# A graph network kernel: edge weights in two scaled 16-bit float parts, and two groups of transfers at other places

## The chip, the cores and the metric

The kernel runs on one core of one Trainium2 chip. The time is device microseconds (us) of one execution, taken in several runs; the number compared is the median. A separate execution was recorded by the hardware profiler, and all rows below come from it.

## What is computed

There are 1250 nodes of 1024 features and 20,000 edges (sorted by destination) with a weight each. Two layers follow one another:

```
h   = relu(layernorm(x))
e   = sigmoid(h @ wenc.T + benc)                      # 1250 x 500
agg = segment_sum((e @ wconv)[src] * weight, dst)     # weighted adjacency times g
x   = x + (agg + e @ wlin.T) @ wdec.T + bdec
h1  = relu(layernorm(x))
z   = h1 @ W.T + b                                    # 1024 x 1024
x   = x + D^-1/2 (A + I) D^-1/2 z                     # A from the edges, unweighted
```

## The kernel before, in words

One core runs five engines from one list of steps that the function schedule() (L138) writes out by hand. Each engine walks through the same list and emits its own part of each step, so the order of steps is the order of work of every engine and of SP's queue of transfers. Semaphores tie the engines together. Nodes are tiled by 128 (10 tiles) and, for the encoder, in 5 blocks of 256.

**Opening.** SP (L688 to L695) loads the heads of the edge rows, six tiles of x, wenc and benc. ScalarE counts where each row of edges starts (L956), GpSimd gathers the edge rows with an indirect transfer (L880). VectorE computes the statistics, ScalarE the norms (L971), TensorE turns the tiles (L1714) and multiplies them with wenc (L1739, L1576 to L1578). Products are made of high and low parts: `product` (L1574) issues three matmuls.

**Edge fields.** On ScalarE the step "parts" (L1049) and on VectorE "fields" (L1239) make of each edge a key (place in a window), the low part of the source and three bf16 parts W1, W2, W3 of the weight, which add up to the f32 weight. TensorE turns the five fields (L1677) into the banks wbank[0], wbank[1] and one of the six dense banks; ScalarE (L1059) and VectorE (L1260) copy them out, each value twice, to kkey, skey and wq.

**Windows.** 50 windows of 25 destinations, each of 5 sub-windows, make the adjacency by matmuls. For window w VectorE ("hot", L1264) compares iotas with kkey and skey, which gives one-hot matrices o_key and o_src, and multiplies the keys with the WPARTS parts of the weight (L1280). TensorE ("win", L1686) then issues for each sub-window, with o_src as the stationary operand:

```
o (100 columns)  += o_src x [ones part | W1 part]     # L1694
o[:, 50:100]     += o_src x W2 part                   # L1696
o[:, 50:100]     += o_src x W3 part                   # L1698
```

ScalarE copies the counts to cnt and the weighted values to stage (L1067, L1070); SP stores stage to adj_scratch in DRAM (L701). Window w on TensorE waits for the stage copy of window w-2 (L1690). The windows are mixed into the dense steps by their due times (L200 to L230): two windows after each encoder group ("e", b, f) from block 1 on, then after each tile of g = e @ wconv ("g", t), then after the first two wlin products ("swl", 0, f). ScalarE and VectorE have their own evacuations and norms beside them, named in `beside` (L182).

**Scales.** Weights and wconv are scaled by powers of two before they become 16-bit parts. The steps ("size", "ew") and ("size", "wc") (L982, L986) sum absolute values on ScalarE, ("limits", "out") and ("limits", "in") send them over DRAM to all partitions (L748, L751), and ("limits", "scale") (L1317) makes the scales on VectorE. The scale of the weights is applied when the adjacency is read back, in "unit" (L1097, L1413).

**W1.** W (the second layer) is sized too: eight tiles of 512 KB are loaded through two buffers (L733) and summed on ScalarE (L978). The list puts sizes 0 to 6 after g tiles 1, 2, 3, 6, 9 and the first two wlin products, the last size at step (1, 1), and the step "bounds" at (1, 5).

**Aggregation.** The 1250 destinations are done in three thirds (500, 500, 250). SP loads the adjacency rows of a third into the one buffer raw ("piece" L786 for the first, "raw" L796 for the others; a load waits until all ten units of the third before are made). ScalarE and VectorE make of each source tile k a pair of 16-bit parts, a unit (ring of 6), and TensorE multiplies it with g ("sk", L1804), after the wlin products of that third. Beside the first third ScalarE and VectorE count degrees (L990, L1430), and SP turns the ten tiles of cnt with turning transfers ("flip", L809). The degree row goes out to DRAM and back ("row", L800) for the row sums of the second third (L1488). The step ("raw", 1) stands behind the last flip.

After that come the decoder, the second layer norm, and the second layer with its own products; the change leaves them alone.

Of the kernel before, what the change touches and what calls it, by code (L numbers as in the profile page):

```python
# [17 lines left out]
P = 128  # L18
T = 10
# [29 lines left out]
WPARTS = 3  # L49
# [15 lines left out]
EW_ROWS = 125.0  # L65
# [8 lines left out]
KEY, SLO, W1, W2, W3 = range(5)  # L74
# [63 lines left out]
def schedule():  # L138
# [35 lines left out]
    steps += [third[3]] + lo(e[1], t1[1], t1[2], t1[3]) + [e[2], ("fields",)] + lo(e[2]) + [("load", "ew"), ("load", "wc"), e[3]] + norms(2)[1:]  # L174
# [3 lines left out]
    def both(block):  # L178
# [4 lines left out]
        (1, 0): turn(2)[:2] + fourth[1:3] + turn(2)[2:], (1, 1): fourth[3:], (1, 2): [("size", "ew"), ("norm", 6)] + fifth[:1], (1, 3): [("norm", 7), ("split", 6), ("turn", 6)],  # L183
# [29 lines left out]
    for i, s in enumerate(dense + [("end",)]):  # L213
        while stream and i >= begin and (stream[0][0] * total <= spent * NW or s[0] == "end"):
            if stream[0][1] == ("hot", 0):

                steps += [("lo", *g) for g in late]
                late = []
# [7 lines left out]
        if s[0] in ("e", "g", "t", "edges") and not by_dma(s):  # L226
            late += [s]
# [7 lines left out]
    for n in range(NS):  # L235
# [4 lines left out]
        for k in range(T):  # L240
# [19 lines left out]
        if n + 1 < NS:  # L260
# [41 lines left out]
def build(nc, x, edge_rows, heads_dst, nat_src, nat_dst, nat_w,  # L302
# [4 lines left out]
    limit_row = nc.dram_tensor("limit_scratch", (P, 2), F32).ap()  # L307
# [17 lines left out]
    for s in STEPS:  # L325
# [7 lines left out]
        elif s[0] in ("t", "e", "g", "z", "edges"):  # L333
# [32 lines left out]
    with ExitStack() as ctx:  # L366
# [23 lines left out]
        kkey = small("kkey", [128, ROWS, 2], BF16)  # L390
        skey = small("skey", [128, ROWS, 2], BF16)
        wq = small("wq", [128, ROWS, WPARTS, 2], BF16)
        iota_s = small("iota_s", [128, 128], BF16)
        a2_rest = at("a2_rest", [P, T, B], F16, 0)
        dis_row = at("dis_row", [P, NODESP], F32, 0)
        assert top[0] >= T * B * 2
        iota_k = small("iota_k", [128, WC], BF16)
# [3 lines left out]
        lane = small("lane", [128, 128], F32)  # L401
# [18 lines left out]
        sizes = small("sizes", [P, 2], F32)  # L420
# [25 lines left out]
        R_X = R_OX + (RING * SUB * (256 + 8 * KC) + 31) // 32 * 32  # L446
        R_END = R_X + 4 * 4096
# [10 lines left out]
        o_key = at("o_key", [128, RING, SUB, 1 + WPARTS, KC], BF16, R_OX + RING * SUB * 256)  # L458
# [1418 lines left out]
```

## Time and profile before

| | us |
|---|---|
| median of 3 runs | 463.74 |
| lowest, highest | 461.7, 467.1 |
| the profiled execution, its own time | 462.57 |
| its span, first to last instruction | 460.8 |
| TensorE busy in it | 451.3 (98%) |
| VectorE, ScalarE busy in it | 309.9 (67%), 239.8 (52%) |

Busy time is the union of an engine's instructions; the ends of matmuls are modelled and overlap the next ones, so the start of the next matmul says more than the duration of one. A row of the timeline has start, duration, engine, line, operation, output and input with shapes, and in brackets how long the engine sat idle before it and what ended that. DMA rows of SP's queue are the issue of a transfer, not the transfer.

### The profile page before, as it was taken

How to read it: one execution, taken by the hardware profiler on the slowest of the kernel's cores; microseconds unless marked ns; L12 is line 12 of the kernel's file. 1: busy time of each engine (PE TensorE's matmuls, PEld its weight loads, DVE VectorE, ACT ScalarE, POOL GpSimd, SP SyncE). 2: the span in 40 equal slices, each digit the busy share in tenths (PEclk: the TensorE clock that was granted, in tenths of full speed). 3: DMA queues.
4: the chain of work that ended last, by engine and by line, in shares of the span. 5: the costliest groups of instructions: out<-in, count | busy, mean ns of one | idle time of the engine just before them, and what ended most of it. 6: DMA issues, size and time to landing. Idle time of an engine off the chain costs nothing.

```text
span 460.8 us, 9335 instructions
## 1 busy us (share of the span) xinstructions
PE 451.3 (98%) x3452; PEld 341.2 (74%) x3452; DVE 309.9 (67%) x603; ACT 239.8 (52%) x452; POOL 42.5 (9%) x63
## 2 busy tenths in 40 slices
PE   7999999998999998999999999999999999999997
PEld 5999999987876455449888887888889944444454
DVE  6999897975965322965867777848563556667652
ACT  6987896639769823314434444546644722222220
POOL 3511200000000000000000000266500000000000
PEclk9999999999999999999999999999999999999999
DMA  8850965297545799143730004350659004423433
GB/s 306 271 179 24 159 104 126 73 342 251 182 152 117 144 80 378 63 123 103 288 102 0 2 0 140 136 183 1 246 212 360 7 1 160 138 91 117 155 134 113
DMA packets 48402, 66.42 MB, mean 144 GB/s; under 512 B 25793, under 2 KB 35024, under 8 KB 46820
## 3 DMA queue, kind: packets, MB, share of 16 engines
q1 hardware_dynamic: 48036, 65.39, 46.7%
q8 instruction: 32, 0.52, 0.5%
q0 software_dynamic: 320, 0.39, 0.4%
q14 instruction: 14, 0.11, 0.1%
HBM read 43.62 MB, written 16.77 MB: 131 GB/s over the span
## 4 chain that ended last, share of the span: by engine, by line
PE 89%; DMA 5%; ACT 2%; SPq 2%; issue 1%; DVE 0%; POOL 0%; POOLq 0%
PE bank L1576 21%; PE bank L1577 20%; PE bank L1578 20%; PE bank L1592 19%; DMA raw<-adj_scratch 3%; PE bank L1694 2%; DMA w_tile<-w 2%; PE bank L1714 1%; SPq L817 1%; PE bank L1739 1%; PE bank L1696 1%; PE bank L1698 1%; DMA adj_scratch<-stage 1%; ACT before L956 1%; PE bank L1654 1%
## 5 line engine op out<-in xcount | busy, mean ns | idle before, releaser
L1592 PE MATMUL bank<-a,h_hi 128*128 128x256 f16 (+3 forms) x400 | 85.5, 270 | 0.0
L1592 PE MATMUL bank<-a,h_lo 128*128 128x256 f16 (+3 forms) x400 | 85.5, 270 | 0.0
L1576 PE MATMUL bank<-right,left 128*128 128x512 f16 (+1 forms) x148 | 54.4, 367 | 0.0
L1578 PE MATMUL bank<-right,left 128*128 128x512 f16 (+1 forms) x148 | 54.4, 367 | 0.0
L1577 PE MATMUL bank<-right,left 128*128 128x512 f16 (+1 forms) x148 | 54.4, 367 | 0.0
L1146 ACT CAST left<-zs 128x512 f16<-128x512 f32 x35 | 21.5, 617 | 60.3 <-PE bank L1578 60.3
L1561 DVE SCALAR_TENSOR_TENSOR x<-bank,dis_u,x 128x512 f32<-128x512 f32 (+2 forms) x37 | 26.7, 722 | 34.2 <-PE bank L1578 34.2
L1576 PE MATMUL bank<-unit,g 128*128 128x500 f16 (+3 forms) x120 | 40.8, 340 | 2.1 <-DVE unit L1418 2.1
L1592 PEld LDWEIGHTS bank<-a,h_hi 128*128 128x128 f16 (+1 forms) x400 | 38.9, 97 | 4.2 <-issue 0.3
L1592 PEld LDWEIGHTS bank<-a,h_lo 128*128 128x128 f16 (+1 forms) x400 | 39.1, 98 | 3.8
L1576 PE MATMUL bank<-h0T,we 128*128 128x256 f32 (+3 forms) x144 | 41.3, 287 | 0.0
L1578 PE MATMUL bank<-unit,g 128*128 128x500 f16 (+3 forms) x120 | 40.7, 339 | 0.0
L1577 PE MATMUL bank<-unit,g 128*128 128x500 f16 (+3 forms) x120 | 40.7, 339 | 0.0
L1577 PE MATMUL bank<-h0T,we 128*128 128x256 f32 (+3 forms) x144 | 40.3, 280 | 0.0
L1578 PE MATMUL bank<-h0T,we 128*128 128x256 f32 (+3 forms) x144 | 40.2, 279 | 0.0
L1418 DVE SCALAR_TENSOR_TENSOR unit<-raw,scales,unit 128x500 f16<-128x500 f32 (+1 forms) x30 | 18.7, 651 | 23.1 <-ACT unit L1106 23.1
L1548 DVE SCALAR_TENSOR_TENSOR right<-whole,o_scales,right 128x512 f16<-128x512 f32 x28 | 26.6, 1014 | 8.7 <-ACT right L1154 8.7
L1576 PE MATMUL bank<-wd_hi,hT 128*128 128x512 f32 (+1 forms) x80 | 31.7, 396 | 0.0
L1577 PE MATMUL bank<-wd_lo,hT 128*128 128x512 f32 (+1 forms) x80 | 31.6, 395 | 0.0
L1106 ACT ACTIVATE unit<-raw,scales 128x500 f16<-128x500 f32 (+1 forms) x30 | 18.5, 650 | 25.1 <-PE bank L1578 14.3
L1578 PE MATMUL bank<-wd_hi,hT 128*128 128x512 f32 (+1 forms) x80 | 31.4, 393 | 0.0
L1694 PE MATMUL bank<-o_key,o_src 128*128 128x100 bf16 x250 | 27.8, 206 | 1.4 <-ACT stage L1070 1.4
(188 smaller groups left out, 1060.5 us busy)
## 6 DMA issues: line engine op xcount, KB each, us to landing
whole<-w SPq DMA_DIRECT2D x7, 1024.0 KB, 7.4
adj_scratch<-stage SPq DMA_DIRECT2D x50, 125.0 KB, 2.1
right_scratch<-right SPq DMA_DIRECT2D x5, 1024.0 KB, 4.0
right<-right_scratch SPq DMA_DIRECT2D x5, 1024.0 KB, 4.8
h<-x SPq DMA_DIRECT2D x9, 512.0 KB, 5.9
x<-x SPq DMA_DIRECT2D x9, 512.0 KB, 5.3
out<-x SPq DMA_DIRECT2D x18, 256.0 KB
w_tile<-w SPq DMA_DIRECT2D x8, 512.0 KB, 5.3
```

What stands on the lines that cost most here:

```text
L817: sp.dma_start(a2[:, :, P * k:P * (k + 1)], cnt[:, k, :], transpose=True).then_inc(flipped, 16)
L956: ins = nc.scalar.activation(before[:, c, :], firsts[:], ACT.Sign, bias=heads[:, c:c + 1])
L1106: nc.scalar.activation(units[0][:, u % UNITS, 0:c].rearrange("p (w d) -> p w d", d=W), raw[:, 0:c // W, k, :], ACT.Copy, scale=scale_of[1] ...
L1146: nc.scalar.copy(left[0][:, nth[p, b] % LEFTS, :, :], side(b, PRODUCTS[p][0])).then_inc(left_hi, 1)
L1418: v.scalar_tensor_tensor(units[1][:, u % UNITS, 0:c].rearrange("p (w d) -> p w d", d=W), raw[:, 0:c // W, k, :], scale_of[1], units[0][:, ...
L1548: v.scalar_tensor_tensor(right[slot_of(i)][1][:, k, :], whole[slot_of(i)][:, k, :], w1_scale, right[slot_of(i)][0][:, k, :], ALU.mult, ALU ...
L1561: v.scalar_tensor_tensor(xs, bank[banks_of[g]][0:n, 0:c.stop - c.start], dis_u[0:n, t:t + 1], xs, ALU.mult, ALU.add).then_inc(bank_free, 1)
L1576: pe.matmul(o, lhs[0], rhs[0], start=first, stop=False, skip_group_check=True)
L1577: pe.matmul(o, lhs[0], rhs[1], start=False, stop=False, skip_group_check=True)
L1578: return pe.matmul(o, lhs[1], rhs[0], start=False, stop=last, skip_group_check=True)
L1592: ins = pe.matmul(o, h1[i][0:n, k, 128 * f:128 * (f + 1)], moving, start=(k == 0 and part == 0 and i == 0), stop=(k == T - 1 and part == p ...
L1694: pe.matmul(o, o_src[:, r, i, :], o_key[:, r, i, 0:2, :], start=(i == 0), stop=False, skip_group_check=True)
```

## The change

- WPARTS is 2: the weight is multiplied by its scale first and then split in two 16-bit float parts. kkey, wq, iota_k and o_key are 16-bit float, o_src and skey stay bf16. The third matmul of each sub-window goes, and so do the fifth turned field, its dense bank and its copy on VectorE.
- The scale of the weights is therefore needed before the fields. The weights are loaded behind the second tile of x; ScalarE sums them before its first norm; SP stores the sums, waits, and loads them to all partitions before its list of steps begins; a step "weights" on VectorE makes the scale, and one on ScalarE the high part. The units use a constant factor instead of the scale. The limits of wconv stay where they were, half as large.
- ("raw", 1) stands in step (0, 7), ahead of ("degrees",), ("row", "out") and flips 7, 8 and 9; flip 7 was before issued with the earlier ones. ("raw", 2) stays.
- W1's sizes 0 to 4 follow g tiles 2, 4, 6, 8 and the first wlin product; sizes 5, 6, 7 stand at steps (1, 1), (1, 2), (1, 3), with the load of the last tile at (1, 1).

```diff
-WPARTS = 3
+WPARTS = 2
...
-    steps += [third[3]] + lo(e[1], t1[1], t1[2], t1[3]) + [e[2], ("fields",)] + lo(e[2]) + [("load", "ew"), ("load", "wc"), e[3]] + norms(2)[1:]
+    steps += [third[3]] + lo(e[1], t1[1], t1[2], t1[3]) + [e[2], ("weights",), ("fields",)] + lo(e[2]) + [("load", "wc"), e[3]] + norms(2)[1:]
...
-    for k, s in enumerate([("g", 1), ("g", 2), ("g", 3), ("g", 6), ("g", 9), *opening[:2]]):
+    for k, s in enumerate([("g", 2), ("g", 4), ("g", 6), ("g", 8), opening[0]]):
         i = dense.index(s) + 1
-        dense[i:i] = [("size", "w1", k)] + [("load", "w1", k + 2)] * (k + 2 < KD)
+        dense[i:i] = [("size", "w1", k)] + [("load", "w1", k + 2)]
...
                 for d in DEGREES[k]:
-                    steps += [("degree", d)] + ([("flip", d)] if d < T - 2 else [])
+                    steps += [("degree", d)] + ([("flip", d)] if d < T - 3 else [])
             if (n, k) == (0, 7):
-                steps += [("degrees",), ("row", "out"), ("flip", T - 2), ("flip", T - 1)]
+                steps += [("raw", 1), ("degrees",), ("row", "out"), ("flip", T - 3), ("flip", T - 2), ("flip", T - 1)]
             if (n, k) == (1, 0):
                 steps += [("row", "in"), ("load", "wd")]
-            if (n, k) == (1, 1):
-                steps += [("size", "w1", KD - 1)]
+            if n == 1 and k in (1, 2, 3):
+                steps += [("size", "w1", KD - 4 + k)] + [("load", "w1", KD - 2 + k)] * (k == 1)
...
-        if n + 1 < NS:
+        if n == 1:
             steps += [("raw", n + 1)]
...
                 sp.dma_start(h0[t][0:tile_rows(t), :], rows(x, t)).then_inc(x_in[t], 16)
+                if t == 1:
+                    sp.dma_start(ew_raw[:], nat_w).then_inc(ew_in, 16)
...
             sp.dma_start(benc_c[:], benc).then_inc(benc_in, 16)
+            sp.wait_ge(ew_sized, 1)
+            sp.dma_start(ew_row, ew_sizes[:]).then_inc(ew_out, 16)
+            sp.wait_ge(ew_out, 16)
+            sp.dma_start(all_limits[:, 0:EP], ew_row.rearrange("q i -> (q i)").unsqueeze(0).broadcast_to([P, EP])).then_inc(ew_sizes_in, 16)
...
             ins.then_inc(before_ready, 1)
+            act.wait_ge(ew_in, 16)
+            nc.scalar.activation(ew_raw[:], ew_raw[:], ACT.Abs, accum_out=ew_sizes[:]).then_inc(ew_sized, 1)
...
-                    nc.scalar.copy(fld[:, W1, :, :], edges[:, :, 2, :].bitcast(F32))
...
+                elif s[0] == "weights":
+                    act.wait_ge(ew_scale_ready, 1)
+                    nc.scalar.activation(weights[:, 0, :, :], edges[:, :, 2, :].bitcast(F32), ACT.Copy, scale=scale_of[1][0:EP, :]).then_inc(weights_hi, 1)
...
-                                         ACT.Copy, scale=scale_of[1]).then_inc(unit_hi, 1)
+                                         ACT.Copy, scale=UNIT_SCALE).then_inc(unit_hi, 1)
...
+                elif s[0] == "weights":
+
+                    dve.wait_ge(ew_sizes_in, 16)
+                    link(v.tensor_reduce(limits[:, 1:2], all_limits[:, 0:EP], AX, ALU.max))
+                    link(v.tensor_scalar(limits[:, 1:2], limits[:, 1:2], LEAST, None, ALU.max))
+                    link(v.tensor_scalar(scales[:, 1:2], limits[:, 1:2].bitcast(I32), EXP_MASK, None, ALU.bitwise_and))
+                    v.tensor_scalar(scales[:, 1:2], scales[:, 1:2], -1.0, float((HALF_EXP + 254) * EXP_ONE), ALU.mult, ALU.add).then_inc(ew_scale_ready, 1)
+                    dve.wait_ge(ew_scale_ready, 1)
...
-                    v.tensor_tensor(r, wt, f[W1], ALU.subtract)
-                    v.tensor_copy(f[W2], r)
-                    v.tensor_tensor(f[W3], r, f[W2], ALU.subtract)
...
-                    v.scalar_tensor_tensor(f[KEY], a, 1.0, sf, ALU.add, ALU.mult).then_inc(fields_ready, 1)
+                    v.scalar_tensor_tensor(f[KEY], a, 1.0, sf, ALU.add, ALU.mult)
+                    dve.wait_ge(weights_hi, 1)
+                    v.scalar_tensor_tensor(weights[:, 1, :, :], wt, scale_of[1][0:EP, :], weights[:, 0, :, :], ALU.mult, ALU.subtract).then_inc(fields_ready, 1)
...
-                        pe.matmul(o[:, KC:2 * KC], o_src[:, r, i, :], o_key[:, r, i, 2, :], start=False, stop=False,
-                                  skip_group_check=True)
-                        ins = pe.matmul(o[:, KC:2 * KC], o_src[:, r, i, :], o_key[:, r, i, 3, :], start=False, stop=(i == SUB - 1),
+                        ins = pe.matmul(o[:, KC:2 * KC], o_src[:, r, i, :], o_key[:, r, i, 2, :], start=False, stop=(i == SUB - 1),
                                         skip_group_check=True)
```

## Rows read from the trace of the kernel before

**Rows 1.** The page, part 1: busy us, share of the span, instructions.
```profile
PE 451.3 (98%) x3452; PEld 341.2 (74%) x3452; DVE 309.9 (67%) x603; ACT 239.8 (52%) x452; POOL 42.5 (9%) x63
```

**Rows 2.** Waits of TensorE: engine, line, waited for: us, times, longest.
```profile
PE bank L1576 <- DVE unit L1418: 2.1, 1, 2.1
PE bank L1694 <- ACT stage L1070: 1.4, 1, 1.4
```

**Rows 3.** TensorE's timeline in two windows: start us, us, line, op.
```profile
45.95 0.22 PE L1694 MATMUL bank<-o_key,o_src 128*128 128x100 bf16 x1
46.00 0.19 PE L1696 MATMUL bank<-o_key,o_src 128*128 128x50 bf16 x1
...
46.06 0.20 PE L1694 MATMUL bank<-o_key,o_src 128*128 128x100 bf16 x1
...
46.45 0.20 PE L1694 MATMUL bank<-o_key,o_src 128*128 128x100 bf16 x1
```

**Rows 4.** TensorE's groups by form: count | busy us, mean ns.
```profile
L1696 PE MATMUL bank<-o_key,o_src 128*128 128x50 bf16 x250 | 27.0, 187 | 0.0
```

**Rows 5.** ScalarE's timeline, 50 to 71 us.
```profile
50.09 0.47 ACT L1039 ACTIVATE hT<-bank,benc_c 128x256 fp32r<-128x256 f32 x1 [1.30 <-PE bank L1578]
...
61.22 0.47 ACT L1070 COPY stage<-bank 128x250 f32<-128x250 f32 x1
...
70.11 0.47 ACT L1039 ACTIVATE hT<-bank,benc_c 128x256 fp32r<-128x256 f32 x1 [1.78 <-PE bank L1578]
```

**Rows 6.** TensorE's timeline, starts of windows 10 and 19.
```profile
61.74 0.22 PE L1694 MATMUL bank<-o_key,o_src 128*128 128x100 bf16 x1
...
78.25 0.20 PE L1694 MATMUL bank<-o_key,o_src 128*128 128x100 bf16 x1
```

**Rows 7.** VectorE's timeline, 77 to 82 us.
```profile
77.56 0.55 DVE L1280 TENSOR_TENSOR o_key<-o_key,wq 128x750 bf16<-128x750 bf16 x1
...
80.47 0.42 DVE L1319 TENSOR_REDUCE limits<-all_sizes 128x2 f32<-128x256 f32 x1
80.92 0.17 DVE L1320 TENSOR_SCALAR limits<-limits 128x2 f32<-128x2 f32 x1
```

**Rows 8.** Timeline of the opening: SP's queue, ScalarE, VectorE, TensorE.
```profile
6.17 0.62 SPq L695 DMA_DIRECT2D benc_c<-benc  x1
...
9.66 2.38 ACT L971 ACTIVATE h<-h,nbias,rstd 128x1024 f32<-128x1024 f32 x2 [2.86 <-DVE nbias L1236]
...
26.24 0.41 DVE L1245 TENSOR_TENSOR er<-edges,fld 125x256 f32<-125x256 f32 x1
...
29.80 0.42 DVE L1256 SCALAR_TENSOR_TENSOR fld<-er,er 125x256 bf16<-125x256 f32 x1
...
30.86 0.72 PE L1679 MATMUL bank<-identb,fld 125*128 125x125 bf16 x10
```

**Rows 9.** DMA issues by line: count, KB each, median us to landing.
```profile
raw<-adj_scratch SPq DMA_DIRECT2D x1, 2500.0 KB, 12.8
...
all_sizes<-limit_scratch SPq DMA_DIRECT2D x1, 128.0 KB, 3.7
...
benc_c<-benc SPq DMA_DIRECT2D x1, 2.0 KB, 13.3
```

**Rows 10.** Timeline around the first W1 size: SP's queue, ScalarE.
```profile
96.04 1.77 SPq L739 DMA_DIRECT2D w_tile<-w  x2
...
103.66 1.06 ACT L981 ACTIVATE w_tile<-w_tile 128x1024 f32<-128x1024 f32 x1 [4.73 <-DMA w_tile<-w]
```

**Rows 11.** Timeline between first and second third: VectorE, SP's queue.
```profile
157.37 0.74 DVE L1418 SCALAR_TENSOR_TENSOR unit<-raw,scales,unit 128x500 f16<-128x500 f32 x1 [0.39 <-ACT unit L1106]
...
167.76 0.58 SPq L685 DMA_DIRECT2D raw<-adj_scratch  x1
...
172.16 0.32 SPq L804 DMA_DIRECT2D dis_row<-row_scratch  x1
...
184.64 1.45 DVE L1494 SCALAR_TENSOR_TENSOR weighted<-cnt,dis_row 128x1250 f16<-128x1250 f16 x1
```

More of the change, by code:

```diff
@@ L73 @@
 EPS = 1e-5
-KEY, SLO, W1, W2, W3 = range(5)
+KEY, SLO, W1, W2 = range(4)
 NODESP = P * T
@@ L182, in schedule @@
     beside = {
-        (1, 0): turn(2)[:2] + fourth[1:3] + turn(2)[2:], (1, 1): fourth[3:], (1, 2): [("size", "ew"), ("norm", 6)] + fifth[:1], (1, 3): [("norm", 7), ("split", 6), ("turn", 6)],
+        (1, 0): turn(2)[:2] + fourth[1:3] + turn(2)[2:], (1, 1): fourth[3:], (1, 2): [("norm", 6)] + fifth[:1], (1, 3): [("norm", 7), ("split", 6), ("turn", 6)],
         (2, 0): [("split", 7), ("turn", 7)] + fifth[1:], (2, 1): [("size", "wc")], (2, 2): both(turn(3)) + [("norm", 8)],
@@ L215, in schedule @@
             if stream[0][1] == ("hot", 0):
-                steps += [("lo", *g) for g in late]
+                steps += [("lo", *g) for g in late] + [("missed",)]
                 late = []
@@ L225, in schedule @@
                 spent += s[0] in ("e", "g", "swl")
-        if s[0] in ("e", "g", "t", "edges") and not by_dma(s):
+        if s[0] in ("e", "g", "t") and not by_dma(s):
             late += [s]
@@ L395, in build @@
         dis_row = at("dis_row", [P, NODESP], F32, 0)
+        iota_k = small("iota_k", [128, WC], F16)
+        lane = small("lane", [128, 128], F32)
         assert top[0] >= T * B * 2
-        iota_k = small("iota_k", [128, WC], BF16)
         ident = small("ident", [128, 128], F32)
@@ L419, in build @@
         minus_half = small("minus_half", [P, 2], F32)
-        sizes = small("sizes", [P, 2], F32)
+        sizes = small("sizes", [P, 1], F32)
+        ew_sizes = small("ew_sizes", [EP, 1], F32)
         w1_sizes = small("w1_sizes", [P, KD], F32)
@@ L462, in build @@
         edges = at("edges", [EP, RG, 3, ROW], I32, R_RAW)
-        er = [at(f"er{i}", [EP, RG, ROW], F32, R_RAW + 3072 + 1024 * i) for i in range(5)]
-        fld = at("fld", [EP, 5, RG, ROW], BF16, R_RAW + 3072 + 1024 * 5)
+        er = [at(f"er{i}", [EP, RG, ROW], F32, R_RAW + 3072 + 1024 * i) for i in range(4)]
+        fld = at("fld", [EP, 2, RG, ROW], BF16, R_RAW + 3072 + 1024 * 5)
+        weights = at("weights", [EP, WPARTS, RG, ROW], F16, R_RAW + 3072 + 1024 * 6)
         heads_i = at("heads_i", [EP, HC], I32, R_RAW + 10752)
@@ L485, in build @@
         gen16 = at("gen16", [EP, CH], BF16, R_H0T + 16384 + 640 * 15)
-        gen_src = [at(f"gen_src{i}", [EP, 128], BF16, R_OX + 256 * i) for i in range(1 + WPARTS)]
+        gen_src = [at(f"gen_src{i}", [EP, 128], BF16, R_OX + 256 * i) for i in range(4)]
         gen_key = at("gen_key", [EP, WC], BF16, R_OX + 1024)
@@ L1676, in _ @@
                     pe.wait_ge(idents, 2)
-                    for i, (o, c) in enumerate(((wbank[0], 0), (wbank[0], ROWS), (wbank[1], 0), (wbank[1], ROWS), (take(s), 0))):
+                    for i, (o, c) in enumerate(((wbank[0], 0), (wbank[0], ROWS), (wbank[1], 0), (wbank[1], ROWS))):
                         for j in range(RG):
-                            ins = pe.matmul(o[:, c + EP * j:c + EP * (j + 1)], fld[:, i, j, :], identb[0:EP, 0:EP],
-                                            start=(c == 0 and j == 0), stop=True, skip_group_check=True)
-                        if i == 3:
-                            ins.then_inc(fields_turned, 1)
+                            if i < W1:
+                                ins = pe.matmul(o[:, c + EP * j:c + EP * (j + 1)], fld[:, i, j, :], identb[0:EP, 0:EP],
+                                                start=(c == 0 and j == 0), stop=True, skip_group_check=True)
+                            else:
+                                ins = pe.matmul(o[:, c + EP * j:c + EP * (j + 1)], weights[:, i - W1, j, :], ident16[0:EP, 0:EP],
+                                                start=(c == 0 and j == 0), stop=True, skip_group_check=True)
                     ins.then_inc(acc_ready, 1)
```

70 lines of the change are left out of this document (32 added, 38 removed).

## The prediction

> **What bounds the kernel now.** I read the page first, then the waits of TensorE, then the timelines around each of those waits. The page gives TensorE 451.3 us busy in a span of 460.8 us, VectorE 309.9 and ScalarE 239.8 [rows 1]. So the time is the length of TensorE's stream plus its few holes: whatever shortens that stream, or closes a hole, counts one for one unless another engine catches up. The waits of TensorE have two holes past the opening: 2.1 us for a unit of the adjacency and 1.4 us for a staged window [rows 2]. Busy time is no price for a small matmul, since the ends overlap: a 50-column one shows as 187 ns [rows 4], but by the starts inside a window the 100-column one takes 50 ns and the two 50-column ones 60 ns together, and a whole window of five such sub-windows 0.50 us (45.95 to 46.45) [rows 3]; so one of 50 columns is 25 to 30 ns. I price matmuls by starts.
>
> **One matmul of each sub-window less.** The window step issues three matmuls per sub-window, the change two: 250 of the form of L1696 go [rows 4]. 250 x 27 ns = 6.75 us, 0.135 us per window. Ends: 25 ns each is 6.2 us, 30 ns is 7.5 us. The stationary stays bf16 and the moving operand becomes 16-bit float; no product with two different 16-bit formats is in this trace, so its rate is bounded by the 27 ns above and by twice that (a rival below). The page "TensorE: Matmul & The Clock Gate" of the Trainium skill (Back-to-back issue gap) puts a stream of weight load and matmul pairs at about 81 ns per matmul at 128 columns; by that the edit would be worth 20 us. The trace disagrees with it: the 100-column matmul takes 50 ns to the next start [rows 3], so the sum does not use it.
>
> Not all of that is kept. Window w waits for the stage copy of window w-2 on ScalarE. Between 50.1 us, where ScalarE waited 1.30 us for TensorE, and 68 us it never waits again until the 1.78 us at 70.11 [rows 5]: it is behind, and the stage copy of window 8 ends at 61.69, 0.05 us before window 10 starts [rows 5, 6]. A faster TensorE only waits there. Windows 4 to 11, eight of them, buy nothing: 8 x 0.135 = 1.1 us off. Then at window 19 VectorE is what is late: its key operation begins at 77.56 and takes 0.55, the window starts at 78.25 [rows 6, 7]. That VectorE work hangs on ScalarE's catch-up, so it moves forward less than TensorE does; 0.45 us off. Kept: 6.75 - 1.1 - 0.45 = 5.2 us. If ScalarE's lag spreads to later blocks the floor is 3.5; if its stretch loosens the ceiling is 6.75.
>
> VectorE's product of keys and weights has 750 elements at 0.55 us [rows 7], once per window. With 500 it should lose up to a third less a fixed part, some 0.13 us each, 6.5 us in all, beside TensorE: priced at nothing except that it keeps VectorE from becoming the next bound. Of the ten turning matmuls of the fields (0.72 us shown for the group [rows 8]) two go: 0.1 us. The copy of the third part on VectorE goes too, in the shade of the wait for ScalarE's copies.
>
> **The opening.** Added: a load of the weights (78 KB) behind two rows of x, an Abs pass on ScalarE, a store and a broadcast load on SP, five operations on VectorE, one on ScalarE. The Abs (under 0.5 us) falls into ScalarE's 2.86 us wait before the first norm at 9.66 [rows 8]; what waits behind it is that norm. It costs something only if the load lands after about 9. The store queues behind all of the opening's loads: the small benc load, issued last at 6.17 [rows 8], took 13.3 us, to about 19.5 us, and the broadcast of the limits took 3.7 [rows 9]. So the broadcast should land at 23 to 24.5; SP stands until then minus 4, and behind it stand the loads of x rows 6 and 7, whose statistics come only after the fields. VectorE gets to the weights at 26.24 [rows 8], some 2 us later than needed. The block of fields took 26.24 to 30.2 [rows 8]. Three operations leave it (about 0.9 us); the reduction and three linked small ones come (a reduction twice as long took 0.42, a small one 0.17 [rows 7], with links about 1.1 us in all), and one more at the end (0.35): fields ready about 0.6 us later, against TensorE's own arrival at 30.86 [rows 8]. I take 0.1 us of new wait. Ends: 0, and 1.5 us if the broadcast comes 1 us late. The page "DMA: Bandwidth & Descriptors" of the Trainium skill (How many engines) says a transfer of 125 partitions runs on 5 of the 16 engines; then 78 KB would hold five of them half as long as an x row does and push the first half of wenc by about 0.6 us. No row here shows it; it would stay inside the 1.5 us.
>
> **W1's sizes later.** The 1.4 us hole at 106 us has this chain: SP issues the W1 tiles at 96.04, ScalarE comes to size the first at 98.93, waits 4.73 us to 103.66 [rows 10], copies the next g bank and only then the windows, and TensorE's window 32 waits for stage 30 [rows 2]. The first size now stands one g tile later (3.8 us): ScalarE reaches it at about 102.7 and waits 1 us, done by 104.8, while the stage that TensorE needs next is already written. Gain 1.4 us (ends 0 and 1.4). Two of the seven sizes leave this stretch, so ScalarE begins the units about 1.1 us sooner. The last three go into the second third; the last tile's load stands behind the 2 MB of wd, so ScalarE may stand until about 190, but the unit behind it is used only at the eighth step. Cost 0; if that cover is gone, whatever the load is late.
>
> **Second third's rows earlier.** SP issued the load at 167.76 [rows 11], behind two turning transfers and the store of dis; it took 12.8 us to land [rows 9], so the next unit could begin at 180.6, and TensorE resumed at about 182.3 after its wait of 2.1 us [rows 2]. Its own condition, the tenth unit on VectorE, was met at 158.1 [rows 11]. Issued then, and given the same 12.8 us, it lands at 171, against a need at about 178.5: 2.1 us saved, ends 0 and 2.1. Three turning transfers and the store of dis are now behind 2.5 MB. The row load (dis_row) was issued at 172.16 [rows 11]; with the big load out of the queue before it I expect about 176, landing before 184. The first row sum ran at 184.64 [rows 11] and the sixth unit of this third queues behind it on VectorE; TensorE wants that at about 192.8 (five steps of 2.5 us from 180.1). Nothing lost.
>
> **Sum.** 5.2 + 0.1 + 1.4 + 2.1 - 0.1 = 8.7 us. The profiled execution took 462.57 us: 453.9. The median of the three runs is 463.74, 1.2 above it (461.7 to 467.1): I forecast 455.0 us. A measurement of this kernel tells about 1%, 4.6 us, from no change.
>
> **Rivals.**
> 1. A hole stays (0.24). One of the two waits does not close: the W1 tile lands later relative to the shortened stream, or the load of rows shares the engines with the turning transfers. For it: the W1 tiles issued at 96.04 were there only at 103.66 [rows 10]. Against: both moves have 1 to 7 us of room. Price 1.4 to 2.1, or up to 3.5: 456.5 to 458.5.
> 2. Windows worth less and a new wait (0.12). ScalarE's lag reaches past 70 us and the opening or the dis_row chain adds 1 to 2 us. Against: ScalarE waits 1.78 us at 70.11 [rows 5]. Gain 2 to 4.5: 459.3 to 461.7.
> 3. The mixed product is slow (0.05), the other side. A bf16 stationary with 16-bit float moving at half rate: a sub-window would take 2 x (50 + 27 - 3) = 148 ns instead of 98, a window 0.25 us more, fifty 12.5 us; with the 3.5 of the holes 9.0 longer: 472.7. It decides from about 0.07 us more per window, where it eats the holes. Against: f32 and 16-bit matmuls of the trace take the same time per column.
> 4. More than forecast (0.07): the windows keep the whole 6.75 us and ScalarE's stretch shrinks: 452 to 453.
> 5. It does not do what it says (0.02): the sub-window stays at 98 ns because the loads of the stationary set its pace: only the holes count, 460.2.
>
> **Chances.** The forecast has 0.50, its own range 453.2 to 456.8. Range for 8 in 10: 452.0 to 460.0, which takes in rival 1, most of 4 and the start of 2. Faster by over 1% (under 459.1) is the forecast, rivals 1 and 4 and a part of 2: 0.82. Within 1%: the rest of 2, and 5: 0.12. Slower: 0.06.
>
> **What would show it.** The window's start-to-start at 0.36 to 0.37 us instead of 0.50, and the VectorE product near 0.41; TensorE's waits without the 1.4 and the 2.1; more wait of TensorE for stage copies between 60 and 68; the row load landed while TensorE is still in its wlin products; ScalarE waiting about 1 us for the first W1 tile and again for the last; fields ready within 0.3 us of TensorE. Wrong would be: a window of 0.49 or more, a wait of TensorE at the fields above 1 us, or one in the second third for a unit behind the first row sum.

## The result, and the profile after

The changed kernel takes 469.79 us (median of 16 runs, 467.82 to 472.69) against 462.61 us (16 runs, 461.7 to 467.1). The ratio is 1.015, with a 95% interval of 1.0127 to 1.0173: 1.5% slower. Forecast were 455.0 us and a gain. The profiled execution took 470.27 us with a span of 468.5.

The page of the changed kernel, parts 1 and 2 (busy us and share of the span; the granted clock in tenths over 40 slices):

```profile
PE 450.7 (96%) x3200; PEld 340.1 (73%) x3200; DVE 301.7 (64%) x604; ACT 237.6 (51%) x452; POOL 42.9 (9%) x62
...
PEclk9997999599999999999999999999999999999999
```

Against [rows 1], 252 matmuls are gone and TensorE is still as busy as before, in a longer span. Some of that busy time is matmuls that ran slower: the clock row has a 7 and a 5.

TensorE's waits in the changed kernel (engine, line, waited for: us, times, longest):

```profile
PE bank L1709 <- ACT stage L1078: 5.4, 2, 4.9
PE bank L1693 <- DVE weights L1271: 4.9, 1, 4.9
```

The 2.1 and the 1.4 us of [rows 2] are gone, as forecast. Two waits of 4.9 us are new. First the one at the fields, in the timeline of the opening (SP's queue, VectorE, TensorE; start us, us):

```profile
6.70 0.62 SPq L704 DMA_DIRECT2D benc_c<-benc  x1
7.37 0.88 SPq L706 DMA_DIRECT2D ew_scratch<-ew_sizes  x1
24.95 0.34 SPq L708 DMA_DIRECT2D all_sizes<-ew_scratch  x1
25.33 3.61 SPq L745 DMA_DIRECT2D h<-x  x4
...
31.18 0.28 DVE L1250 TENSOR_REDUCE limits<-all_sizes 128x1 f32<-128x125 f32 x1 [4.79 <-DMA all_sizes<-ew_scratch]
...
35.95 0.60 PE L1693 MATMUL bank<-identb,fld 125*128 125x125 bf16 x4 [4.91 <-DVE weights L1271]
```

SP issues the half-kilobyte store of ew_sizes at 7.37 and stands until it has landed, 17.6 us later. The broadcast takes 6.2 more, so VectorE starts at 31.18, not 26.24 [rows 8], and TensorE waits until 35.95.

The second (SP's queue, then ScalarE, then TensorE):

```profile
73.19 0.58 SPq L761 DMA_DIRECT2D limit_scratch<-sizes  x1
73.82 0.91 SPq L714 DMA_DIRECT2D adj_scratch<-stage  x2
74.83 2.61 SPq L740 DMA_TRANSPOSE h16T<-x  x2
77.49 1.07 SPq L714 DMA_DIRECT2D adj_scratch<-stage  x2
83.95 0.33 SPq L765 DMA_DIRECT2D all_sizes<-limit_scratch  x1
...
84.90 0.39 ACT L1078 COPY stage<-bank 128x250 f32<-128x250 f32 x1 [6.87 <-DMA adj_scratch<-stage]
...
85.35 0.26 PE L1709 MATMUL bank<-o_key,o_src 128*128 128x100 f16 x1 [4.90 <-ACT stage L1078]
```

Window 16 waits for the stage copy of window 14, and that for the store of window 10, whose stage buffer (of four) it takes. Issued at 73.82, the store landed at 84.9. The DMA issues of the changed kernel (count, KB each, us to landing) and the stage stores issued from 70 to 78 us:

```profile
limit_scratch<-sizes SPq DMA_DIRECT2D x1, 0.5 KB, 10.7
row_scratch<-dis SPq DMA_DIRECT2D x1, 5.0 KB, 14.2
bound_scratch<-bounds SPq DMA_DIRECT2D x1, 1.0 KB, 3.2
```

```profile
DMA to landing us min/median/max: 10.9/11.1/11.3
```

With its 4 bytes per partition the limits' store took 10.7 us; before, with 8 bytes, 3.3. The same list of the kernel before:

```profile
limit_scratch<-sizes SPq DMA_DIRECT2D x1, 1.0 KB, 3.3
row_scratch<-dis SPq DMA_DIRECT2D x1, 5.0 KB, 11.1
```

What the two waits did to the clock is in a table of windows (window, its us, then busy us of TensorE, weight loads, VectorE, ScalarE, GpSimd, then granted clock, DMA share, GB/s):

```profile
30.00:40.00 10.00, 5.09 (x33) 4.66 (x33) 7.28 (x23) 5.96 (x13) 0.00 (x0) 0.75 0.92 294
40.00:50.00 10.00, 10.00 (x87) 9.95 (x86) 7.76 (x19) 5.08 (x10) 1.86 (x7) 0.91 0.02 5
80.00:90.00 10.00, 4.56 (x36) 4.13 (x36) 2.88 (x9) 4.79 (x13) 0.00 (x0) 0.63 0.89 91
90.00:100.00 10.00, 10.00 (x109) 9.89 (x109) 7.58 (x27) 4.65 (x15) 0.00 (x0) 0.85 0.24 78
```

Before, all four stretches were at 1.00. After each wait TensorE ran for a time at the lower of its two levels (1.2 GHz, half speed). Matmuls of the encoder of one shape, 226 columns, start 0.21 us apart at 87.7 and 0.12 apart at 93.7:

```profile
87.73 0.41 PE L1590 MATMUL bank<-h0T,we 128*128 128x226 f32 x1
87.94 0.41 PE L1591 MATMUL bank<-h0T,we 128*128 128x226 f32 x1
...
93.69 0.28 PE L1590 MATMUL bank<-h0T,we 128*128 128x226 f32 x1
93.81 0.27 PE L1591 MATMUL bank<-h0T,we 128*128 128x226 f32 x1
```

The windows did become shorter. The last two (TensorE) and VectorE's product, with its mean in ns:

```profile
146.10 0.22 PE L1709 MATMUL bank<-o_key,o_src 128*128 128x100 f16 x1
146.15 0.19 PE L1711 MATMUL bank<-o_key,o_src 128*128 128x50 f16 x1
146.18 0.20 PE L1709 MATMUL bank<-o_key,o_src 128*128 128x100 f16 x1
...
146.47 0.20 PE L1709 MATMUL bank<-o_key,o_src 128*128 128x100 f16 x1
```

```profile
L1291 DVE TENSOR_TENSOR o_key<-o_key,wq 128x500 f16<-128x500 f16 x50 | 20.7, 413 | 0.0
```

A window takes 0.37 us, not the 0.50 of [rows 3], and the product 0.41, not 0.55. Here a bf16 stationary with a 16-bit float moving operand is not slow: a sub-window takes 74 ns.

Starts of windows in us, from the timelines of four kernels (the last two are experiments below):

```
window   before   after   moves_alone   both_8_bytes
0         42.01   49.62      41.81         42.82
14        69.91   76.67      69.71         69.88
18        77.53   92.64      77.33         77.44
32       106.01  117.88     104.21        103.09
49       136.94  146.47     135.06        131.68
span      460.8   468.5      456.8         453.7
```

Before to after: 7.6 us are lost by window 0, 8.4 more from 14 to 18 (15.97 against 7.62), and 5.6 are regained from there to window 49. (A further 0.9 is regained between windows 0 and 14 and 1.8 behind window 49, where the 2.1 us wait was; in sum the span is 7.7 longer.)

### The profile page after: what moved, and what is told of

Read it like the earlier page. It is cut to its first block, busy times and chain, and to the rows that moved or that the text cites. A ratio compares the mean times of both kernels' runs of the same rounds, so it can differ in the third digit from the quotient of the medians.

```text
span 468.5 us, 8833 instructions
## 1 busy us (share of the span) xinstructions
PE 450.7 (96%) x3200; PEld 340.1 (73%) x3200; DVE 301.7 (64%) x604; ACT 237.6 (51%) x452; POOL 42.9 (9%) x62
## 4 chain that ended last, share of the span: by engine, by line
PE 84%; DMA 7%; ACT 4%; DVE 2%; SPq 2%; issue 1%; ACTq 0%
PE bank L1589 21%; PE bank L1590 20%; PE bank L1591 20%; PE bank L1605 18%; DMA ew_scratch<-ew_sizes 4%; DMA h16T<-x 2%; PE bank L1709 2%; DMA all_sizes<-ew_scratch 1%; PE bank L1711 1%; SPq L697 1%; PE bank L1727 1%; ACT stage L1078 1%; ACT h L982 1%; ACT cnt L1075 1%; ACT h0T L1029 1%
## 5 line engine op out<-in xcount | busy, mean ns | idle before, releaser
L1589 PE MATMUL bank<-h0T,we 128*128 128x256 f32 (+3 forms) x144 | 42.8, 297 | 0.5 <-DVE h0T L1310 0.5
L1590 PE MATMUL bank<-h0T,we 128*128 128x256 f32 (+3 forms) x144 | 41.7, 289 | 0.0
L1591 PE MATMUL bank<-h0T,we 128*128 128x256 f32 (+3 forms) x144 | 41.5, 288 | 0.0
L1589 PEld LDWEIGHTS bank<-h0T,we 128*128 128x128 f32 (+1 forms) x144 | 28.3, 196 | 0.7 <-DVE h0T L1310 0.7
L1591 PEld LDWEIGHTS bank<-h0T,we 128*128 128x128 f32 (+1 forms) x144 | 28.3, 196 | 0.0
L1590 PEld LDWEIGHTS bank<-h0T,we 128*128 128x128 f32 (+1 forms) x144 | 28.3, 196 | 0.0
L953 POOL TENSOR_TENSOR x<-x,bt 128x1024 f32<-128x1024 f32 (+1 forms) x10 | 25.6, 2556 | 27.5 <-ACT bt L1171 27.5
```

Source lines behind the costliest of these rows:

```text
L953: nc.gpsimd.tensor_tensor(x1[t][0:n, :], x1[t][0:n, :], bt[0:n, :], ALU.add).then_inc(xo_ready, 1)
L1589: pe.matmul(o, lhs[0], rhs[0], start=first, stop=False, skip_group_check=True)
L1590: pe.matmul(o, lhs[0], rhs[1], start=False, stop=False, skip_group_check=True)
L1591: return pe.matmul(o, lhs[1], rhs[0], start=False, stop=last, skip_group_check=True)
```

## Experiments

The theory: both waits come from the two stores whose rows shrank to 4 bytes, or are new with 4 bytes. Rivals: the loads ahead in the opening make the first late; the shifted phase of turning transfers against stage stores makes the second. In all, 15 kernels ran; "before" was timed beside each (medians from 461.55 to 463.51 us), and the ratios are to that. Differences to the changed kernel compare medians of different sittings, so a part of them, up to about 1 us, can be that drift.

**1. The moves alone.** `before` with the changed places of `("size", "w1", k)`, `("load", "w1", k)`, `("raw", 1)` and `("flip", d)`, nothing else.

> The kernel before with the two moves alone: W1's sizes later, and the second third's adjacency rows issued after the tenth unit. Three weight parts, no scale in the opening. If the forecast's terms for the moves (1.4 + 2.1 us) hold, about 3.5 us less than before, near 459.1 us against 462.6, and TensorE's waits without the 2.1 and the 1.4 us. Rival: the holes close only because the changed kernel is late elsewhere (ScalarE and the queues had more room), and alone the moves give under 1.5 us. If the moves do harm of their own (the turning transfers of the last x rows, the store of dis), the time would be at or above 462.6.

Measured: 458.51 us, ratio 0.9918 (0.990 to 0.9936). TensorE's old waits of 1.4 and 2.1 us are gone, the span is 4.0 us shorter. This part of the forecast holds for the moves by themselves.

**2. A constant scale.**

```diff
-            sp.dma_start(ew_row, ew_sizes[:]).then_inc(ew_out, 16)
-            sp.wait_ge(ew_out, 16)
-            sp.dma_start(all_limits[:, 0:EP], ...).then_inc(ew_sizes_in, 16)
-                    link(v.tensor_reduce(limits[:, 1:2], all_limits[:, 0:EP], AX, ALU.max))
+                    link(v.memset(limits[:, 1:2], 128.0))
```

> The changed kernel with a constant 128 as the limit of the edge weights in place of the measured one: no store of ew_sizes, no broadcast of it; the load of the weights, the Abs pass and the split in two parts stay (so the scale is not made from the data). Theory A: both stalls of the changed kernel hang on that round trip, the one at the fields directly (4.9 us and then a lower granted clock, window 0 7.6 us late) and the one at 85 us through the shifted phase of the stage stores against the turning transfers; then both go and the time is near the forecast, 453.5 to 455.5 us, granted clock near 1.00. Theory B: the stall at 85 us belongs to the limits' store, now 4 bytes per partition (10.7 us to land, 3.3 before) and stays: 458 to 462 us with a wait of 4 to 7 us of TensorE for a stage copy between windows 14 and 18. Theory C: window 0 stays late for another reason (the second part's operation behind ScalarE's copy): a wait at the fields of over 1 us stays.

Measured: 461.83 us, 8.0 less than the changed kernel. Window 0 starts at 42.55, but the second wait stays at 4.7 us, the limits' store at 11.4. Theory B, with the time in its range: the stalls are two. The shifted phase isn't the cause, since the opening is on time here.

**3. ew_scratch with 8 bytes per partition.** `ew_row` is (EP, 2), `ew_sizes` [EP, 2] with zeros in the second column, the broadcast reads 250 numbers.

> The changed kernel with ew_scratch two numbers wide (the second is zero): the store writes 8 bytes per partition in place of 4, the broadcast reads twice as much. Theory A: a store of 4 bytes per partition is what lands late (17.5 us for ew_scratch; 10.7 for limit_scratch against 3.3 when it had 8 bytes): with 8 bytes it lands some 8 us after its issue or as the loads ahead of it end, about 19 us, the broadcast at 24, and the 4.9 us at the fields go: 457 to 462 us. Theory B: the store's landing is set by the loads ahead of it in the queues or by something else of the opening, the bytes of a row don't matter: landing within 1 us of 24.9, time within 1.5 us of the changed kernel (469.8).

Measured: 462.59 us, 7.2 less. The store landed 14.3 us after its issue, at 21.48, VectorE began at 27.43, and 1.2 us of the wait remain. Of the late landing of 24.95, the loads ahead account for the time up to about 20 (benc, issued last before it, landed at 19.8), the 4-byte rows for about 3.5 us more. This is nearer to theory A, but the landing moved by 3.5 us where A had it at about 19, and the time is 0.6 above A's range: both theories had a part of the cause.

**4. limit_scratch with 8 bytes per partition**, in the same way; ew_scratch as changed.

> The changed kernel with limit_scratch two numbers wide again (8 bytes per partition, the second is zero), all else as changed. Theory A: the 4-byte store at 73 us stands in the way of the stage stores behind it; with 8 bytes it lands in 3 to 4 us and the wait of 4.9 us for the stage copy at 85 us goes, with the lower clock after it: 461 to 464 us. Theory B: that wait comes from the phase of the turning transfers against the stage stores, shifted by the stall of the opening; then the store's landing may shrink, but the wait stays at 4 to 5.5 us and the time within 1.5 us of 469.8.

Measured: 460.40 us, 9.4 less. The store landed in 5.2 us and the stage stores from 70 to 78 us so:

```profile
DMA to landing us min/median/max: 3.4/3.9/5.0
```

The second wait is gone, and the time is under the range expected. The opening's wait is still there, at 3.9 us in this execution, and window 0 starts at 47.59, so phase is excluded from this side too.

**5. Both with 8 bytes.**

> The changed kernel with both stores (ew_scratch and limit_scratch) 8 bytes per partition. Alone, the one took 7.2 us off the changed kernel and the other 9.4. Theory A, two separate stalls with one cause each: the savings add, 453 to 454 us, and TensorE's waits hold neither the 4.9 us at the fields (1.2 stays) nor the one at the stage copy. Theory B, one shared cause (the phase): the second saving is small, 458 to 460 us.

Measured: 455.68 us, ratio to before 0.9872 (0.9836 to 0.9909): 5.9 us faster than before. The page, TensorE's waits and the clock row:

```profile
PE 443.7 (98%) x3200; PEld 332.6 (73%) x3200; DVE 301.1 (66%) x604; ACT 237.7 (52%) x452; POOL 41.6 (9%) x64
...
PEclk9999999999999999999999999999999999999999
```

```profile
PE bank L1699 <- DVE weights L1277: 0.8, 1, 0.8
...
PE bank L1715 <- ACT stage L1084: 0.5, 1, 0.5
```

One number more per partition in each of two small stores is worth 14.1 us by the medians, 14.8 by the spans and 13 by the two ratios (1.015 and 0.9872). The two theories had 453 to 454 and 458 to 460 us; the time is in neither range and nearer to A. Both waits went, as A had it, but the savings don't add in full: 7.2 and 9.4 alone, 14.1 together. A part of this is that the opening's wait varies from one execution to the next (3.9 us in limit_8_bytes, 4.9 in the changed kernel, 5.6 in experiment 8, all with the same 4-byte store).

**6. The scale without DRAM.** limit_scratch with 8 bytes, the store of ew_sizes and its broadcast gone, and (excerpt):

```diff
-UNIT_SCALE = 2.0 ** -7
+UNIT_SCALE = 1.0
+            pe.wait_ge(ew_sized, 1)
+            pe.matmul(wbank[0][:, 2 * ROWS + 1:2 * ROWS + 2], ew_sizes[:].broadcast_to([EP, 128]),
+                      ones[0:EP, 0:1], start=True, stop=True, ...).then_inc(ew_sizes_in, 1)
             pe.wait_ge(rstd_ready, 1)
```

> The changed kernel with the limit of the edge weights made on the chip: one f32 matmul of the 125 partition sums against a column of ones in TensorE's opening gives the sum on all 128 partitions, in place of the store and the broadcast; since the sum bounds the adjacency's entries, UNIT_SCALE is 1. limit_scratch has 8 bytes per partition. Theory A: the scale is ready before VectorE comes to the weights, SP loads x rows 6 and 7 some 10 us earlier, no wait at the fields above 0.5 us: 452 to 454 us. Theory B: the operations on the fields themselves (the second part behind ScalarE's copy of the first) are what is late: a wait of 1 us or more at the fields stays, 454.5 to 457 us.

Measured: 454.54 us, ratio 0.9838 (0.9803 to 0.9872), the fastest kernel measured here. No wait at the fields is left, yet window 0 starts at 43.03: in this execution the first norm began at 10.92 us, 1.1 later than with the moves alone. The wait is theory A's, the time is just inside theory B's range, and from 455.68 the intervals don't part it.

**7. That norm.** The load of the weights goes behind all opening loads, the Abs pass behind the copies of the parts, the ones matmul behind the last turning of block 1.

> As ones_matmul, but the load of the weights stands behind all other opening loads, the Abs pass behind the three copies of the parts on ScalarE, and the ones matmul behind the last turning of block 1 on TensorE. In ones_matmul the load stood ahead of x rows 2 to 5 and wenc and the first norm began at 10.92 us (9.83 with the moves alone). Theory A: that load was pushing the whole opening, so window 0 starts at 41.8 to 42.3 us instead of 43.0 and the time is 453.0 to 454.3 us. Theory B: the 1.1 us was the spread of one execution, window 0 is late by the 0.6 to 1.2 us of VectorE's longer block of fields, and the time is that of ones_matmul within 0.5 us.

Measured: 455.42 us. Neither theory: TensorE now waits 1.5 us for the Abs pass, so the order costs what it could have gained. Whether the load's old place delays the norm stays open; in both_8_bytes, with that same place, the norm begins at 9.73.

**8. SP's wait moved.** `("limits", "in")` goes from (3, 1) to (3, 3).

> The changed kernel (4-byte stores both) with SP's broadcast load of the limits, and the wait for their store ahead of it, two encoder groups later in SP's order. Theory A: the stall at 85 us comes because SP stands at that wait (from 78.6 to 83.9 us) with the stage store of window 14 behind it, and the stage copy of window 16... waits for a free stage buffer; then the long landing of the store is covered, and the wait of 4.9 us goes though the store still takes 10 to 12 us: 460 to 464 us. Theory B: the DMA queues themselves are held up by the 4-byte store; then the stage stores are late wherever SP stands, and the time stays at 467 to 470 us.

Measured: 468.67 us. Theory B. SP no longer stands at the broadcast, but the wait for the stage copy is still 4.1 us: the stage stores issued from 70 to 78 us took 9.4 to 10.2 us to land.

**9. 4 bytes, spaced.** `limit_row` is (P, 2), of which `[:, 0:1]` is stored and read.

> The changed kernel with limit_scratch two numbers wide, of which only the first of each pair is written and read: still 4 bytes per partition, 8 bytes apart. Theory A: the size of the piece that a partition writes (4 bytes) makes the store late: it lands in 10 to 12 us and the time is that of the changed kernel, 468 to 471 us. Theory B: 4-byte neighbours in DRAM are what is slow: spaced, it lands in 3 to 6 us and the time is 460 to 462 us.

Measured: 496.09 us, and neither range: the strided broadcast of 128 x 128 single numbers, which I had not thought of, took 42.2 us and gave TensorE a wait of 32.7. The store itself shows what was asked:

```profile
all_sizes<-limit_scratch SPq DMA_DIRECT2D x1, 64.0 KB, 42.2
...
limit_scratch<-sizes SPq DMA_DIRECT2D x1, 0.5 KB, 5.2
```

Just as many bytes, 8 bytes apart, land like rows of 8 bytes, as in theory B. It isn't the size of the piece but how near its neighbours are.

**10 and 11. The cost by itself.** both_8_bytes with one more store ahead of the limits', `sp.dma_start(extra_row, sizes[:, 0:1])`, waited for by nobody; `extra_row` is (P, 1) in the first, the first column of (P, 2) in the second.

> The kernel both_8_bytes with one more store ahead of the limits': 4 bytes of each of 128 partitions to an array of its own that nothing reads, and nothing waits for it, its numbers next to each other in DRAM. Theory A: such a store holds up what is behind it in the queues: the turning transfers and the stage stores land late, limit_scratch takes over 8 us, a wait of TensorE for a stage copy of 3 us or more is back between windows 14 and 18, 459 to 464 us. Theory B: only the wait for the store's own end was the cost: then nothing but 0.6 us of SP's time is added, 455 to 456.5 us.

> The kernel both_8_bytes with the same extra store of 4 bytes per partition, its numbers 8 bytes apart in DRAM. In limit_spaced such a store landed in 5.2 us. Theory A, neighbours within DRAM are what is slow: no hold-up, 455 to 456.5 us. Theory B, 4-byte pieces are slow wherever they lie: as extra_touching, 459 to 464 us.

Measured: 462.28 us touching, 455.75 apart. The DMA issues of the first and of the second:

```profile
extra_scratch<-sizes SPq DMA_DIRECT2D x1, 0.5 KB, 9.0
limit_scratch<-sizes SPq DMA_DIRECT2D x1, 1.0 KB, 8.6
```

```profile
extra_scratch<-sizes SPq DMA_DIRECT2D x1, 0.5 KB, 4.0
limit_scratch<-sizes SPq DMA_DIRECT2D x1, 1.0 KB, 3.8
```

Theory A touching, theory A apart. Touching, the store holds up what is behind it: stage stores issued from 70 to 78 us land in 8.4 us (3.1 in both_8_bytes), and TensorE's wait for a stage copy is back at 3.3. So a store nobody waits for costs 6.6 us.

**12. The same in a quiet place**, ahead of the bounds' store at 187 us.

> The kernel both_8_bytes with the extra store of 4 bytes per partition, neighbours in DRAM, not at 66 us but at 187 us, ahead of the store of the bounds; both_8_bytes has no turning transfer and no stage store there, and the store of the bounds (8 bytes per partition) took 3.4 us to land. Theory A: the store is slow by itself: it lands in 9 to 12 us and the bounds' store behind it in 8 us or more. Theory B: it is slow only with other traffic behind it (the turning transfers of 500 rows of 256-byte pieces), as at 66 us: here both land in 3 to 4 us. The time stays at 455 to 457 us by either, since the raw load behind it has slack.

Measured: 455.11 us; the extra store landed in 7.5 us, the bounds' behind it in 7.3 (3.4 without). Between the theories: it is slow by itself, and slower still (9.0 to 11.4 us) with the turning transfers about.

**13. The size of the row.** Six stores there, one after the other.

> The kernel both_8_bytes with six extra stores at 187 us, ahead of the bounds' store, each waited for before the next is issued: 4, 8, 16, 32 and 64 bytes of each of 128 partitions, rows next to each other in DRAM, and last 4 bytes of each partition, 8 bytes apart. Nothing reads them; SP stands the longer for them, so the time is not that of a kernel to use. Theory A, what counts is how many partitions' pieces share a short stretch of DRAM: the landing falls with the row (about 7 us at 4 bytes, 3 to 4 at 8, 2 to 2.5 from 16 on) and 4 bytes apart land like 8. Theory B, something is special with 4 bytes alone: 8 to 64 bytes land alike, and 4 bytes apart as late as 4 bytes touching.

One execution (469.89 us, with SP standing at the stores), with 0.5, 1, 2, 4 and 8 KB for rows of 4 to 64 bytes:

```profile
extra_scratch<-all_sizes SPq DMA_DIRECT2D x1, 0.5 KB, 7.3
extra_scratch<-all_sizes SPq DMA_DIRECT2D x1, 1.0 KB, 3.0
extra_scratch<-all_sizes SPq DMA_DIRECT2D x1, 2.0 KB, 1.4
extra_scratch<-all_sizes SPq DMA_DIRECT2D x1, 4.0 KB, 1.4
extra_scratch<-all_sizes SPq DMA_DIRECT2D x1, 8.0 KB, 1.4
apart_scratch<-all_sizes SPq DMA_DIRECT2D x1, 0.5 KB, 3.0
```

Theory A, though from 16 bytes on faster than its 2 to 2.5 us. The sixteenfold store lands five times as fast, and 4 bytes 8 apart land like 8 bytes.

The page "DMA: Bandwidth & Descriptors" of the Trainium skill (Specifications) says that below 512 bytes a transfer is handled by reading, changing and writing back. Rows from 16 to 64 bytes are below that too and land in 1.4 us, so the rule alone doesn't give the step; that neighbours in one stretch of DRAM wait for each other would fit both, and is argued here, not shown.

**14. TensorE fed in the stall.** The changed kernel with 42 matmuls of 250 columns, which nobody reads, ahead of `pe.wait_ge(fields_ready, 1)`.

> The changed kernel with 42 matmuls of 250 columns ahead of TensorE's wait for the fields, on data that nothing reads: the stall at 31 to 36 us stays, but TensorE is busy in it. If the lower granted clock of the slices after it (0.75 and 0.91) follows TensorE's idling and costs some 2.5 us, window 0 starts at 47 to 47.5 us instead of 49.6 with a granted clock near 1.00 from 30 to 50 us, and the time is 467 to 468 us. If the clock falls for another reason, window 0 stays at 49.6 or later and the time at 469.5 to 471 us.

Measured: 467.02 us, 2.8 less than the changed kernel. They ran from 31.85 to 36.34, window 0 starts at 47.38, and the stretch from 36 to 50 us is at a clock of 1.00. From the fields' matmuls to window 0 are 11.04 us, against 13.67 in the changed kernel (35.95 to 49.62) and 11.00 in both_8_bytes (31.82 to 42.82): the clock cost 2.6 us there. (Window 0 gains only 2.2, as the unused matmuls outlast the fields by 1.0.)

```profile
36.00:50.00 14.00, 14.00 (x139) 13.78 (x138) 12.34 (x31) 10.10 (x21) 1.87 (x7) 1.00 0.18 60
...
PE bank L1711 <- ACT stage L1078: 3.5, 2, 3.0
PE bank L1589 <- DVE h0T L1310: 2.3, 1, 2.3
```

The second stall is not shorter in this run: its wait for the stage copy is 3.0 us and one of 2.3 for h0T follows it, where the changed kernel has 4.9 and 0.5. Nothing was fed into that one, so that its lower clock has the same cause is taken over from here.

**15. The parts without the moves.** both_8_bytes with the old places of W1's sizes and of the rows.

> The kernel both_8_bytes with W1's sizes and the second third's adjacency rows where the kernel before has them: the two weight parts alone, both stores 8 bytes per partition. If the parts' term and the moves' term add, both_8_bytes (455.7) plus what the moves gave alone (3.5 to 4.0) is 459.2 to 459.7 us, 0.5% faster than before. If the shorter windows make the old holes longer (TensorE reaches them 3 to 4 us sooner and the W1 tiles and the raw rows come when they came), it is 460.5 to 463 us: then the parts alone are worth nothing and only the pair pays.

Measured: 459.47 us, ratio 0.9939 (0.992 to 0.9958). The moves take 3.8 us off it and took 3.8 off the kernel before, so in sum the terms add. The parts of the sum don't. TensorE's waits and one stretch of 5 us behind the longer one:

```profile
PE bank L1715 <- ACT stage L1084: 2.9, 2, 2.3
PE bank L1595 <- DVE unit L1437: 0.3, 1, 0.3
...
105.00:110.00 5.00, 4.45 (x29) 3.69 (x30) 2.60 (x7) 4.81 (x13) 0.00 (x0) 0.66 0.80 236
```

The hole at the first W1 tile is 2.3 us where it was 1.4 [rows 2]: shorter windows alone do lengthen it. Behind it the granted clock falls to 0.66, which it didn't in the kernel before, and windows 32 to 34 take 5.30 us against 3.53 in both_8_bytes. So that hole costs 4.1 us. The hole of 2.1 us at the second third is 0.3 without any move: the load of rows landed in 10.5 us here, 12.8 before. By spans the later W1 sizes are worth 1.7 us alone and 4.3 with the parts (windows 19 to 49: 57.60 against 53.34), the earlier rows 2.1 alone and 0.2 with the parts (behind window 49: 322.24 against 322.02). That both sums are 3.8 us is chance as far as these runs show; why the rows landed sooner is open.

## Why the prediction was wrong

**Where it failed.** The step is "The opening", which I put at 0.1 us with ends 0 and 1.5, and with it the whole class of cost of a small store. Two readings were at fault.

First, "the broadcast should land at 23 to 24.5". I let the store cost nothing behind benc's landing (19.5) and gave the broadcast 3.7. The store needed until 24.95, the broadcast 6.2. With 8-byte rows (both_8_bytes) it was 21.4 and 5.5: 26.9, and a wait of 0.8 to 1.2 us, inside my ends. So the queue of loads would have fitted the range; the 4-byte rows took it out. The trace of before had a hint, and I didn't read it: among its DMA issues the store of dis, 5 KB in 4-byte pieces, took 11.1 us where the bounds' 1 KB took 2.7. Turning transfers stand around that store, and no run takes the two apart there. I called dis_row's place safe and passed over why its store was slow.

Second, the limits' store, which I gave no term, as its bytes were halved. It went from 3.3 to 10.7 us, and TensorE waited 4.9 us for a stage copy behind it. I priced a transfer by its bytes and by who waits for it; here the stage stores that merely follow it in the queues are what counted.

**What it cost**, by spans, changed kernel against both_8_bytes: 14.8 us. Up to window 0 it is 6.8: 4.1 of wait and 2.6 of lower clock. From window 14 to 18 it is 8.4 (15.97 against 7.56): 4.9 of wait, and the other 3.5 fall in the stretch of the clock of 0.63 and 0.85. The stretch after that is 0.4 shorter. I had no clock term at all. The two waits of 4.9 us cost 2.6 and up to 3.5 us more here, and the one of 2.3 us in no_moves 1.8 more; the 2.6 is shown by fed_hole, the others are read from stretches at the lower clock.

**What held, and the size of what was off.**

- Windows: forecast 6.75 issued, 5.2 kept. From window 0 to 49, both_8_bytes takes 88.86 and moves_alone 93.25: 4.4 kept. From window 19 to 49 it is 3.7, or 0.123 each (forecast 0.135); from 0 to 19 it is 0.7 where the forecast gives 1.0. Of that, windows 4 to 12 keep 0.2 and windows 12 to 19 nothing. In both_8_bytes TensorE waits 0.5 us for a stage copy at window 10 and 0.4 for o_key at window 19, the two places read in [rows 5, 6, 7].
- Opening without the slow store: 1.0 us (42.82 against 41.81), not 0.1: 0.8 of it the wait at the fields.
- W1's sizes and the second third's rows: forecast 1.4 + 2.1 = 3.5, measured alone 1.7 + 2.1, and 3.8 (0.9918 of before) in time, 4.0 in span. With the parts it is 4.3 + 0.2 (experiment 15), so the split that I added up is not the one that the changed windows have. ScalarE waits 0.88 us for the first tile in moves_alone, forecast 1, and 1.94 in both_8_bytes.
- So the sum with 8-byte stores is 4.4 + 4.0 - 1.0 = 7.4, and the spans say 7.1, for a forecast of 8.7; the medians say 5.9 (455.68 against 461.55). That 455.68 is only 0.7 from the 455.0 that I gave for the change as it stands is partly luck: I counted from 463.74, the median of three, and the kernel before has 462.61 in 16 runs and 461.55 beside this one.
- Small readings: a sub-window before is 100 ns (0.50 / 5), not the 98 of rivals 3 and 5; five steps of 2.5 us from 180.1 end at 192.6, not 192.8. "The same time per column" is true to 8%: at 256 columns f32 matmuls start 0.118 us apart and 16-bit ones 0.109. None of these changes the sum.
- The rivals: the mixed product isn't slow (3); no old hole stays (1). The mechanism that happened was on no list, though "a wait of TensorE at the fields above 1 us" was named as what would prove the forecast wrong. The 0.06 for slower was too little for an edit that adds a round trip through DRAM ahead of TensorE and narrows another.

## What to carry to other kernels

Look at the row size of every small store to DRAM, and where a change narrows one, treat it as a new instruction: padding 4-byte rows to 8 bytes cost nothing that the traces show and was worth 13 to 14 us here. Rows of 16 bytes landed faster still, measured alone only. Spacing the numbers helps the store as much, but not where they are read back at that pitch. Price a store also by what follows it in the queues, not only by who waits for it. Where a wait of some us on TensorE is in question, look for time after it at half clock: the waits of 4.9 us and the 2.3 us of no_moves were followed by it, the 1.4 and 2.1 us of the kernel before were not. And when two terms are added, check what each is worth in the presence of the other.

## What the hardware showed that I had not expected

- A store of one f32 from each of 128 partitions to neighbouring addresses took 7.3 us alone and 9.0 to 11.4 us among turning transfers. Alone, 8-byte rows took 3.0, 16 to 64 bytes 1.4, 4 bytes at a pitch of 8 took 3.0; among turning transfers 8-byte rows took 3.3 to 5.4 and 4 bytes at a pitch of 8 took 4.0 and 5.2.
- Such a store delays what is behind it: an 8-byte store from 3.4 to 7.3 us, stage stores of 125 KB from 3.1 to 8.4 and 11.1.
- Reading the other way is dearer: a broadcast of 128 x 128 single numbers at a pitch of 8 bytes took 42.2 us, of the same numbers without gaps 3.2 to 4.9.
- After idling 4.9 us TensorE's granted clock was 0.75 and 0.91, or 0.63 and 0.85, in the next 10 us stretches; fed with unused matmuls it stayed at 1.00. After idling 2.34 us (no_moves) it was 0.66 in the 5 us from 105 on.
